# Two transposes and two copies of the first frame moved ahead, and four gathers tied to them, in a DLRM tower on one core

## The reference

```python
e = stack([tbl_f[ids[:, f]] for f in range(16)], axis=1)      # 2048 x 16 x 256
xk = e
for i in range(3):
    z = einsum('bfe,bge->bfge', e, xk)                        # all pairs of features
    z = relu(einsum('bcl,oc->bol', z.reshape(...), Ws[i]) + bs[i])
    z = sum(z, axis=-1); outs.append(z)                       # 2048 x 16
    xk = broadcast(z over the 256 elements)
h = concat([outs..., dense_ctx])                              # 64 features
y = relu(relu(h @ W_top1 + b_top1) @ W_top2 + b_top2) @ W_top3
```

## Time and profile before

| | |
|---|---|
| median of 3 runs | 581.73 us (577.67 to 581.93) |
| profiled execution | 579.74 us, its span 578.0 us |
| granted TensorE clock, mean | 0.956 of full speed |
| instructions | 10773 |
| indirect gathers on GpSimd | 256, mean 970 ns |
| transposes on TensorE | 512 matmul instructions, mean 288 ns |

### The profile page before, as it was taken

One profiled execution on the slowest core, in us unless ns is written; L12 is line 12 of the kernel. 1 busy time (PEld: TensorE's weight loads), 2 busy tenths in 40 slices (PEclk: granted clock), 3 DMA queues, 4 the chain that ended last, 5 costly groups with the idle time before them and its releaser, 6 DMA issues.

```text
span 578.0 us, 10773 instructions
## 1 busy us (share of the span) xinstructions
PE 476.3 (82%) x3990; PEld 190.8 (33%) x3990; DVE 542.8 (94%) x326; ACT 498.7 (86%) x1471; POOL 467.8 (81%) x354
## 2 busy tenths in 40 slices
PE   5559888687888798878989788798869888789988
PEld 5213233232333333232333323233333323233324
DVE  1697999999999999999999999999999999999994
ACT  1143698999999999999999999989999999999875
POOL 6665888889888888888888889888888888888630
PEclk9689898999989989998999999799999989999979
DMA  3352212221222122212221222212212212210000
GB/s 98 92 145 74 75 56 57 63 64 56 74 58 64 56 71 72 67 56 74 62 64 56 69 60 61 73 57 82 64 56 66 61 60 74 57 54 1 1 2 0
DMA packets 14334, 35.43 MB, mean 61 GB/s; under 512 B 5493, under 2 KB 5879, under 8 KB 14266
## 3 DMA queue, kind: packets, MB, share of 16 engines
q0 software_dynamic: 12288, 33.57, 20.3%
q1 hardware_dynamic: 1994, 1.17, 0.8%
HBM read 34.71 MB, written 0.01 MB: 60 GB/s over the span
## 4 chain that ended last, share of the span: by engine, by line
DVE 38%; ACT 28%; PE 18%; issue 10%; POOL 3%; another core or an unknown queue 1%; DMA 1%; ACTq 0%; DVEq 0%; POOLq 0%
DVE prod L436 32%; ACT outer L637 15%; PE z_ps L827 8%; DVE outer L485 6%; ACT outer L627 3%; ACT sq L582 3%; POOL x_rows L342 3%; PE t_ps L790 3%; ACT relu L593 2%; ACT xt L574 2%; PE turn_ps L898 1%; PE turn_ps L902 1%; PE turn_ps L860 1%; PE zs_ps L842 1%
## 5 line engine op out<-in xcount | busy, mean ns | idle before, releaser
L436 DVE TENSOR_TENSOR prod<-t_ps,xt 128x2048 f32<-128x2048 f32 x190 | 420.8, 2281 | 11.0 <-remote 6.7
L342 POOL DMA_INDIRECT x_rows<-in_tbl,ids_sb x256 | 248.4, 970 | 73.1 <-issue 62.0
L637 ACT ACTIVATE outer<-outer,bias_sb 128x256 f32<-128x256 f32 x476 | 236.7, 518 | 3.0 <-DVE outer L485 3.0
L827 PE MATMUL z_ps<-prod,w_sb 128*32 128x512 f32 x1520 | 191.2, 622 | 37.3 <-DVE prod L436 34.3
L356 POOL TENSOR_TENSOR intra<-xt 128x1024 f32<-128x1024 f32 (+4 forms) x90 | 205.1, 2281 | 6.0 <-PE z_ps L827 4.5
L574 ACT ACTIVATE xt<-t_ps 128x512 f32<-128x512 f32 x128 | 75.2, 604 | 45.2 <-PE t_ps L790 21.7
L637 ACT ACTIVATION_READ_ACCUMULATOR outer<-outer,bias_sb 128x1 f32 x476 | 100.2, 210 | 0.0
L485 DVE TENSOR_TENSOR outer<-y_ps,z_all 128x1408 f32<-128x1408 f32 (+2 forms) x60 | 93.4, 1598 | 4.5 <-ACT outer L627 3.5
L790 PE MATMUL t_ps<-ident,x_rows 128*128 128x128 f32 x512 | 81.2, 288 | 19.0 <-DMA x_rows<-in_tbl,ids_sb 7.1
L827 PEld LDWEIGHTS z_ps<-prod,w_sb 128*32 128x32 f32 x1520 | 45.8, 111 | 124.8 <-issue 93.3
L790 PEld LDWEIGHTS t_ps<-ident,x_rows 128*128 128x128 f32 x512 | 55.9, 143 | 81.8 <-issue 59.6
(11 more groups left out here) (69 smaller groups left out, 219.1 us busy)
## 6 DMA issues: line engine op xcount, KB each, us to landing
x_rows<-in_tbl,ids_sb POOLq DMA_INDIRECT x256
w_sb<-in_w SPq DMA_DIRECT2D x1, 512.0 KB
feat<-in_dense SPq DMA_DIRECT2D x1, 128.0 KB
w_sb<-in_w SPq DMA_DIRECT2D x1, 128.0 KB
ids_sb<-in_ids SPq DMA_DIRECT2D x1, 120.0 KB
ident<-in_identity SPq DMA_DIRECT2D x1, 64.0 KB, 2.1
w_sb<-in_w0t SPq DMA_DIRECT2D x1, 64.0 KB
sel_sb<-in_sel SPq DMA_DIRECT2D x1, 48.0 KB
```

Of the source, the lines that this page charges most:

```text
L342: pool.indirect_dma_start(out=x_rows[:, par, f, :], out_offset=None, in_=tables[f], in_offset=bass.IndirectOffsetOnAxis(ap=ids_sb[:, NF * ...
L436: dve.tensor_tensor(prod[:, m % PROD_RING, half, :].rearrange("p (f g s) -> p f g s", f=QF, g=QF), t_ps[:, tbank(b, q, half), :, :].unsque ...
L637: act.activation(outer_of(b)[:, o // OP, o % OP, :], outer_of(b)[:, o // OP, o % OP, :], ACT.Relu, bias=bias12_sb[:, layer - 1, o:o + 1], ...
L827: mm = pe.matmul(z_ps[j * GR:(j + 1) * GR, m % 2, 0:n], w0_sb[:, half, slot, :], src[:, half, j * n:(j + 1) * n], start=(slot == 0 and hal ...
```

## The change

Three edits, all in the order of work. No computation is added or taken away.

On TensorE, in frame 0 only, the transposes of (1,1,0) and (1,1,1) are issued after the contraction of u3 and ahead of `form_yt`; before, they stood after the contraction of u4, as they still do in the other frames. On ScalarE, in frame 0 only, the copies of these two tiles are ahead of the rectification of pair 2 (u3, u4). On GpSimd, the gathers of quad 3 of batch 1 (features 12 to 15) wait for the transpose of (1,1,1) where they waited for the contraction of u2 of batch 0, and the gathers of quad 0 of batch 2 behind them no longer have a wait for the transpose of (1,0,1) of their own (inside `gather` they wait for the transpose that frees their buffer, tile (0,0,1), which is long done).

```diff
@@ gpsimd @@
             gather(1, 2 * QF, 3 * QF)
-            pool.wait_ge(contracted, part(0, "u2") + 1)
+            pool.wait_ge(transposed, tile(1, 1, 1) + 1)
             gather(1, 3 * QF, NF)
-            pool.wait_ge(transposed, tile(1, 0, 1) + 1)
             gather(2, 0, QF)
@@ scalar @@
                 rectify(b, 1)
-                rectify(b, 2)
+                if b > 0:
+                    rectify(b, 2)
                 copy_tile(b + 1, 1, 0)
                 copy_tile(b + 1, 1, 1)
+                if b == 0:
+                    rectify(b, 2)
                 move_yt(b)
@@ tensor @@
                 contract(b, "u3")
+                if b == 0:
+                    transpose_tile(1, 1, 0)
+                    transpose_tile(1, 1, 1)
                 form_yt(b)
                 contract(b, "u4")
-                transpose_tile(b + 1, 1, 0)
-                transpose_tile(b + 1, 1, 1)
+                if b > 0:
+                    transpose_tile(b + 1, 1, 0)
+                    transpose_tile(b + 1, 1, 1)
                 sum_pairs(b, 0)
```

## The result

The changed kernel took **583.11 us** (median of 22 runs, 578.47 to 586.26) against 580.30 of the kernel before (22 runs, 576.12 to 582.60), taken side by side: a ratio of 1.0058, with a 95% interval of 1.0037 to 1.0078, or about +3.4 us (the medians differ by 2.8). That is under the 1% that was called no change, and within 0.4 us of the number forecast. The forecast was 1.8 us above the 581.73 then on record, so a part of this nearness comes from the kernel before being 1.4 us faster here. The profiled execution took 583.20 us with a span of 581.4, 3.4 more than the span before, so this trace can be read for a difference of that size. It does not show the path forecast.

What follows compares the result with a forecast made beforehand. GpSimd was taken as full, with VectorE following it from about batch 8 to 11. +4.0 - 1.2 = +2.8 us on the profiled 579.74 gave 582.5, plus 1.0 toward the median: 583.5, range 579.5 to 587.5.

Steps and rivals of the forecast that it cites:

- The gap of 3.56 us: VectorE's idle time before batch 1's first multiply, waiting for tile (1,1,0)'s copy; forecast to go, multiply near 51.7.
- VectorE's third multiply, "-0.8 us": Batch 1's third multiply on VectorE waits for transpose (1,2,0)'s copy, leaving 0.5 to 1.2 us gained; taken as -0.8.
- 2.8 as a bound: Transpose (1,1,1) might be seen up to 2.8 us after its modelled end, putting GpSimd's net shift at up to 5.6.
- GpSimd's first inner product at 60.4, +4.0: Batch 1's first inner product, queued behind eight gathers starting at 50.5, moves from 56.45 to near 60.4: +4.0 us.
- 1.2 us absorbed in two waits: GpSimd's waits for i0 contractions at 88.38 and 122.97 (0.64 and 0.81 us) disappear, absorbing 1.2 us of its shift.
- Lateness 4.3 at batch 3: GpSimd's last product's end minus the next batch's first VectorE multiply start: 0.69 us before, 4.3 or a little more forecast.
- VectorE stalls in batches 4 to 6: VectorE stalls following late GpSimd until itself 2.8 us behind its old times, swallowing its -0.8.
- the +2.8 of the sum: GpSimd's stream shift, +4.0 less 1.2 absorbed, becoming a 2.8 us later end of the kernel.
- A: Rival: VectorE bounds, so its gap's 3.56 us or the remaining 0.8 are gained: 578.2 or 580.9; chance 0.14.
- B: Rival: transpose (1,1,1) seen 2.8 us late, GpSimd's first inner product after about 63.5, 588.6, over 1% slower; chance 0.09.
- C: Rival: lateness of batches 3 to 5 is absorbed and VectorE has hidden room at batch 9; 581.7, no change; chance 0.17.

Runs made afterwards that it cites:

- split: Changed kernel with gathers (2,0) to (2,3) moved behind batch 1's first inner product; 580.47 us, ratio 1.0011 to the kernel before.
- order_only: Kernel before with only the TensorE and ScalarE reordering, GpSimd's gathers keeping their old waits; 578.84 us, ratio 0.9984.
- direct: Changed kernel with its eight gathers replaced by eight direct DMAs of the same size from SyncE, fetching wrong rows; 577.84 us, ratio 0.9964.
- gathers_only: Kernel before with only the gathers' waits changed, TensorE and ScalarE in the old order; 583.81 us, ratio 1.0034.
- pool_again: Kernel before with GpSimd making batch 1's first i1 product a second time into the same place; 581.70 us, ratio 1.0034.
- order_sooner: Kernel before with the TensorE and ScalarE reordering and only the buffer wait ahead of gathers (1,8) to (2,3); 587.44 us, ratio 1.0121.
- after_less: Changed kernel with GpSimd's first i1 product of batch 1 cut to 32 of 384 columns; 579.94 us, ratio 1.0012 to the kernel before.

## Why the prediction was right in its number and wrong in its path

*The gap of 3.56 us goes.* Right: the multiply is at 51.84 against 51.7 forecast, the copies at 48.94.

*VectorE's third multiply, "-0.8 us".* Wrong, and this is the step that failed: it is +2.7. Its inputs on TensorE were even early: transpose (1,2,0) ended at 56.94 against 57.9 forecast. What was mis-sized is the hand-over, put at 0 from the one row where it was seen at once, while the other row showed 2.8 us. I kept 2.8 as a bound, gave it to the wrong transpose, and explained it by whether TensorE had paused. The two rows differ in something else, which the earlier trace rows show: the first transpose ended at 45.68, with gathers issued until 46.76; the second at 56.85, 2.8 us behind the last gather. The change puts gathers under the second. (The old gap of 3.56 us looks in part like the same delay: the pair sums ended at 51.92+0.64 = 52.56 and were seen at 54.02, with gathers until 54.07. In split they are seen at once, although its gathers run to 54.15, so gathers beside a result are not enough by themselves.) Removing their tie (order_only, 0.9984), thinning them (split, -2.8 at the third multiply) or replacing them (direct, -2.7) each undoes the delay; gathers_only makes it alone in its trace. That the tie of the gathers costs the time is shown, since the interval of order_only (0.9951 to 1.0017) and that of the changed kernel (1.0037 to 1.0078) don't meet; by what the gathers delay TensorE's results is not shown.

*GpSimd's first inner product at 60.4, +4.0.* At 61.80, +5.4. The gathers ended at 60.25 where 60.2 was forecast (they began 0.9 us sooner, and one took 1.88 us); the rest is i0, which was itself handed on late.

*1.2 us absorbed in two waits.* The first vanished. The second stood (0.70), since GpSimd there waits for a TensorE that follows a VectorE which is itself 4.2 us late.

*Lateness 4.3 at batch 3, VectorE stalls in batches 4 to 6.* Not in this kernel: lateness 0.87, and VectorE's shift is +4.2 at batch 4 and +4.0 at batch 7. Both streams are late by the same amount, so GpSimd has nothing to impose. The mechanism exists; split shows it with lateness 5.83 and 3.6 us lost between batches 4 and 7, and pool_again agrees. It did not act here. That the +2.8 of the sum is near the measured +3.4 is luck: 2.7 and 1.5, with 0.5 lost on the way to batch 14 and 1.3 given back in the tail, happen to come near it.

*The collision.* Not in the prediction at all. In the trace before, the two are 0.12 us apart. The Trainium skill, SBUF — State Buffer, Who interferes with whom, says that a VectorE instruction with two SBUF inputs contends with a GpSimd instruction that reads SBUF, that the pair of ports they share is locked, and that the one issued first holds it. That they contend, the traces show: +1.46 us where GpSimd's product takes 1.28. On who waits they agree in order_only, where GpSimd's product begins at 84.62 and VectorE's second at 84.83 and takes 1.77 us instead of 0.69. They don't in the changed kernel, where VectorE's product begins first by 0.3 us and is the one that stands; there the measurement decides, as far as starts on GpSimd can be read that closely. The same section says that DMA never contends with a compute engine and that TensorE waits on nobody. With direct DMAs the trace agrees (0.07 us for u5 at 174 GB/s); with gathers TensorE's results come 4.8 and 7.5 us late, and no run here shows whether a port has part in that.

*The rivals.* A had the right engine: VectorE does bound, and a piece of its gap is worth having. direct kept 1.5 to 2.3 us of the 2.7 it gained, with an interval just below 1. In the changed kernel the delay took it back and more. B put the transpose lag as a price of GpSimd's stream, on the other transpose, which was on time; it would have decided past 63.5, and 61.80 was reached. C is excluded by an interval above 1.

## What to carry to other kernels

Before moving gathers, write down which TensorE results fall under them, and price each hand-over by rows with gathers and rows without, apart: one early example of "at once" is no price. Where VectorE and GpSimd both read their two inputs from SBUF, look at how far their products lie apart, since a shift of 3 us can turn a near miss into a collision. And where a number comes out right, check the lines that should have shown its path: here lateness at one batch told that it was another.

## What the runs showed of the hardware

- TensorE's results reached waiters up to 4.8 us late (changed kernel), 4.6 (gathers_only) and 7.5 us late (order_sooner) while GpSimd issued a run of gathers. In the changed kernel, with gathers from 49.61 to 60.25, the pair sums that end at 53.35 are seen at once, u5, which ends at 55.06, is 2.3 us late, and i0 and the transpose are seen 1.5 us after the last gather. In gathers_only and order_sooner the late results were seen before the last gather was over. Eight direct DMAs of the same size did not do it to u5 (0.07 us).
- While results were late, TensorE's rows broke off for 0.79 and 0.27 us inside one run of sums that waited for nothing (changed kernel, 57.3 to 58.8).
- VectorE's three inner products took 2.97 to 3.44 us instead of 1.89 in nine kernels where a GpSimd product began beside them, and 1.89 in after_less, where only gathers did. A gather beside them took up to 1.88 us on GpSimd instead of 0.95 (changed kernel, at 50.87), though the two of after_less took 0.98 and 0.95.
- The tail ran at a granted clock of 0.50 for 6.8 us in one execution (before) and at 1.00 in the same part of another (after), whose tail was 1.3 us shorter.
